# Delta inputs, first group: memsets ahead of the first gathers, second group's gathers behind the first group's power

## The reference, cut to what matters

```python
x = x + _L0_attn_ref(_layernorm(x, axis=-1), ...)
x = x + _L0_ffn_ref(_layernorm(x, axis=-1), ...)     # out = sum(weights * y of the 2 chosen experts)
x = x + _L1_attn_ref(_layernorm(x, axis=-1), ...)    # q, k, v = silu(short_conv(x @ Wq, ...)) and so on
x = x + _L1_ffn_ref(_layernorm(x, axis=-1), ...)
```

## Time and profile before

| | |
|---|---|
| median of 3 runs | 1436.7 us (1435.37 to 1441.69) |
| the profiled execution | 1436.34 us |
| its span, first to last instruction | 1434.6 us |
| busy in the span | TensorE 89%, VectorE 57%, GpSimd 35%, ScalarE 32% |
| clock granted to TensorE, mean | 0.916 of full speed |

### The profile page before, as it was taken

The page is one execution under the profiler, slowest core; times in us unless marked ns, Lnnn a source line. Parts: engine busy times, 40 slices in busy tenths (PEclk is TensorE's granted clock), DMA queues, the critical chain, the costliest instruction groups (busy, mean ns, idle before and its releaser), DMA issues. The chain is left out here.

```text
span 1434.6 us, 36334 instructions
## 1 busy us (share of the span) xinstructions
PE 1277.0 (89%) x12853; PEld 951.4 (66%) x12854; DVE 820.7 (57%) x1882; ACT 463.3 (32%) x1085; POOL 496.5 (35%) x709
## 2 busy tenths in 40 slices
PE   7999999899999999838888887298999999889997
PEld 5888888767776777614554555287888888746565
DVE  6788889533222222248888877457566666435443
ACT  1211222132222222226767774011222222123332
POOL 4344666415411111065666432223343434210000
PEclk9999999889999999968888997558999999779999
DMA  9999910113311211122444434612643334000001
GB/s 309 349 370 340 328 49 31 38 48 109 113 59 60 64 59 59 48 73 95 138 122 119 114 107 136 129 50 74 117 115 89 94 94 147 2 0 30 29 22 37
DMA packets 219962, 156.60 MB, mean 109 GB/s; under 512 B 111744, under 2 KB 201344, under 8 KB 219840
## 3 DMA queue, kind: packets, MB, share of 16 engines
q1 hardware_dynamic: 204288, 129.11, 30.7%
q0 software_dynamic: 9312, 25.44, 5.4%
q10 hardware_dynamic: 6240, 0.39, 0.3%
HBM read 64.47 MB, written 90.44 MB: 108 GB/s over the span
## 5 line engine op out<-in xcount | busy, mean ns | idle before, releaser
L945 PE MATMUL ps_sc<-w,a_qeo 128*128 x568 | 183.1, 466 | 0.0
L753 DVE TENSOR_TENSOR a_stm<-a_vpad,ps_sc 128x352 f32<-128x352 f32 x71 | 37.0, 521 | 177.2 <-ACT a_vpad L517 177.2
L945 PEld LDWEIGHTS ps_sc<-w,a_qeo 128*128 128x128 f32 x568 | 104.0, 193 | 46.5 <-issue 2.5
L423 POOL DMA_DIRECT2D x_slots<-a_stm x66 | 36.4, 551 | 226.1 <-issue 226.1
L1585 PE MATMUL d_pp<-d_xT,d_w_p 128*128 128x512 f32 x192 | 112.1, 732 | 1.1 <-ACT d_xT L1320 1.1
L1477 DVE SCALAR_TENSOR_TENSOR d_cout<-d_cin,d_taps,d_cout 128x512 f32<-128x512 f32 x144 | 106.1, 747 | 6.1 <-ACT d_cout L1338 2.7
L915 PE MATMUL ps_kv<-w,a_stm 128*128 x426 | 105.7, 384 | 1.2 <-DVE a_stm L746 1.1
L915 PEld LDWEIGHTS ps_kv<-w,a_stm 128*128 128x128 f32 x426 | 79.2, 190 | 30.1 <-issue 12.5
L2328 PE MATMUL g_pp<-g_xT,g_w_g 128*128 128x512 f32 x192 | 90.8, 613 | 8.3 <-ACT g_xT L2219 8.3
L1253 POOL DMA_INDIRECT got<-x_slots,d_idx x64 | 75.5, 1180 | 18.7 <-issue 16.1
L517 ACT ACTIVATE a_vpad<-ps_sc 128x352 f32<-128x352 f32 x71 | 33.0, 464 | 140.0 <-PE ps_sc L945 140.0
(11 more groups left out here) (273 smaller groups left out, 2834.4 us busy)
## 6 DMA issues: line engine op xcount, KB each, us to landing
x_slots<-a_zeros SPq DMA_DIRECT2D x32, 1024.0 KB, 11.0
rec<-d_kve SPq DMA_DIRECT2D x32, 384.0 KB, 2.9
u_kve<-rec SPq DMA_DIRECT2D x32, 384.0 KB, 3.9
a_qeo<-x_slots SPq DMA_DIRECT2D x71, 128.0 KB, 2.0
x_slots<-a_stm POOLq DMA_DIRECT2D x66, 128.0 KB, 2.1
rec<-d_act_out SPq DMA_DIRECT2D x32, 256.0 KB, 3.7
u_qkT<-rec SPq DMA_DIRECT2D x32, 256.0 KB, 3.5
w<-in_w SPq DMA_DIRECT2D x4, 1408.0 KB, 14.0
```

What stands on the lines that cost most here:

```text
L753: dve.tensor_tensor(e_h[:, q, 0:HID], e_gate[:, q, :], ps_3[q], ALU.mult).then_inc(h_out, 1)
L945: mm = pe.matmul(ps, e_xT[:, q, k, :], w13[:, s, k, bass.ds(e_hidden, 1), :], start=(k == 0), stop=(k == KD - 1))
```

## The change

Two things in GpSimd's program of `delta_inputs`. The four memsets stand ahead of the first group's index copy and gathers. And in step 0 the gathers of tiles 0 and 1 of group 1, with their index copy, stand behind the shift and the power of group 0; those of tiles 2 and 3 follow them as before (in step 0 nothing lies between). The later steps are as they were.

```diff
-            gather(0, 0, (0, 1, 2, 3))
             pool.memset(power[:, :, 0, :], -0.5).then_inc(zeroed, 1)
             pool.memset(power[:, :, 1, :], 0.5).then_inc(zeroed, 1)
             pool.memset(cin[:, :, :, 0:HIST], 0.0).then_inc(zeroed, 1)
             pool.memset(s_rows[:, 0:HIST], 0.0).then_inc(zeroed, 1)
+            gather(0, 0, (0, 1, 2, 3))
             pool.wait_ge(zeroed, 4)
 
             def step(i, par):
                 u, q = i - 1, 1 - par
                 v = i - 2
-                if has(i + 1, NG):
+                if i > 0 and has(i + 1, NG):
                     gather(i + 1, 1 - par, (0, 1))
                 if has(i, NG):
                     pool.wait_ge(mom_done, GROUP * (i + 1))
...
                     pool.tensor_scalar(shifted[:, :], mom[:, :, 1], EPS, None, ALU.add).then_inc(shift_done, 1)
                     pool.wait_ge(shift_done, i + 1)
                     pool.tensor_tensor(rstd[:, :], shifted[:, :], power[:, :, 0, 0], ALU.pow).then_inc(rstd_done, 1)
+                if i == 0:
+                    gather(1, 1, (0, 1))
```

## The result

The changed kernel took 1440.54 us in the median of 22 runs (1436.84 to 1443.86), the kernel before 1438.32 in 22 (1433.14 to 1442.64). The ratio is 1.0019, with a 95% interval of 1.0011 to 1.0027: 2.7 us slower, 1.6 to 3.9 (the two medians lie 2.2 apart). The forecast was 1439.4, or 2.7 us slower, and no difference that one measurement tells apart.

What follows compares the result with a forecast made beforehand. GpSimd's queue was taken to bound the restart: VectorE waits for group 1's eighth gather, whose landing moves from 635.55 to 638.21. That +2.66 us, with nothing absorbed, made the median 1439.4 us; range 1433.0 to 1446.5.

Steps and rivals of the forecast that it cites:

- The bound: At the start of delta inputs, GpSimd's gather queue is late; VectorE idles 5.60 us until group 1's eighth gather lands.
- The sum, term by term: GpSimd's queue to VectorE's adds of group 1: eighth gather starts at 635.35, lands at 638.21, against 635.55: 2.66 us later.
- The memsets: Four memsets ahead of group 0's gathers on GpSimd: first gathers move back by 0.34 us, with 0 as other bound.
- The gathers beside VectorE's adds: Group 0's late gathers on GpSimd, now running while VectorE adds, take 0.14 us more.
- The lead is lost: Group 0's normalisation comes 2.68 us earlier, but VectorE's late adds of group 1 hold up its convolutions, so nothing is gained.
- No slack behind: Behind VectorE's adds of group 1, nothing absorbs the delay: every later row of the stage comes 2.7 us later.
- The rule on contention: GpSimd gathers contend with VectorE's two-input instructions; by this rule savings and costs of moved gathers sum within 0.2 us.
- Lead kept: Rival, chance 0.14: VectorE's adds of group 1 don't bound the restart, group 0's 2.68 us carry to the end; 1434.0 us.
- absorbed: Rival, chance 0.11: a later join, such as the 3.87 us wait for the decay, absorbs the delay; 1436.7 us.
- Clock, slower: Rival, chance 0.13: shifted work meets one more drop of TensorE's clock, 7.0 us, giving 1446.4 us.
- clock, faster: Rival, chance 0.06: one drop of TensorE's clock vanishes, 7.0 us less, giving 1432.4 us.
- one dip: One stretch of lowered TensorE clock, priced at 7.0 us from matmul counts in 1000 to 1020 and the next 20 us.

Runs made afterwards that it cites:

- The wait by tile: Changed kernel, with VectorE waiting for group 1's gathers tile by tile instead of once for all eight; ratio to before 0.9969, and 0.9984 when measured again.
- the order alone: Kernel before, with only group 1's gathers of tiles 0 and 1 moved behind group 0's power, memsets left in place; ratio to before 1.0035.
- the pure delay: Kernel before, with a GpSimd memset of 3072 elements per partition and a wait for it ahead of the first gathers; ratio to before 1.0010.
- the memsets alone: Kernel before, with only the four memsets moved ahead of group 0's gathers, group 1's gathers in their old order; ratio to before 0.9983.

## Why the prediction held

*The bound.* Read from rows 3 and rows 4: VectorE's wait ends with the eighth gather of group 1. The row of after names the DMA again, for 10.58 us, and 637.72 is 2.83 behind the start of the eighth gather at 634.89 (2.86 before).

*The sum, term by term.* The mechanism held, and the closeness of the terms is in part luck, since two errors of opposite sign nearly cancel. The memsets were put at 0.34 us; they delay the first gather by 0.14 (+0.93 in place of +0.79). The four and the start of the copy take 0.20, since instructions of 0.10 to 0.14 us overlap, and the gap between copy and gather shrinks a little; the value lay between the bounds 0 and 0.34. The gathers beside VectorE's adds were put at 0.14 more and cost 0.25 (610.19 to 619.32 is 9.13, not 8.88), nearly all in the one at 615.33, 1.18 us, which runs beside VectorE's work on tile 0. The delay of 0.20 us too much and the 0.11 too little nearly cancel: eighth gather predicted at +10.15 (619.80), measured +10.06. Fourth tile's add +13.01, measured +13.02. Shift +14.75, measured +14.88. First gather of group 1 +16.58, measured +16.69; the eighth +25.70, measured +25.63. Adds of group 1 +28.56, measured +28.46. The delay was predicted as 2.66 and is 2.56 in the first pair of profiles, 2.49 in the second.

*The lead is lost.* Right, and on the path named, ScalarE's waits for VectorE's convolutions. It starts to be lost two waits earlier than the one at 654.73 that the prediction named: the first is at 643.22. The wait by tile shows its cause directly.

*No slack behind.* Right in rows: a delay of 2.40 us arrived whole at the shift of group 2, and the 5.33 us of the order alone as well. In time it is shown only within 1.5 us or so. Behind group 2 the rows don't show it as cleanly. From its shift to the delta rule the second profile of before took 248.97 us, the pure delay 249.99, the changed kernel 250.06 and 250.13, the order alone 250.55, but the memsets alone, which are early, 249.75 as well. Whether a delay grows there by about 1 us is open.

*The rule on contention.* The prediction read two of the four gathers beside group 0's adds in before (0.98 and 0.94 us) and left out this one:

```profile
622.36 1.11 POOL L1253 DMA_INDIRECT got<-x_slots,d_idx  x1 [0.30 <-issue]
```

So of the eight gathers beside these adds in the two kernels, two took 1.11 and 1.18 us and the others 0.94 to 0.98. The Trainium skill (GPSIMD Engine Reference, section 8, Key points) names this contention; beside the adds the runs show at most 0.25 us of it in the sum. Elsewhere in the stage gathers take longer. In before, the first two behind the decay of group 0 lie beside VectorE's two-input product (line 1513) and its scan (line 1519):

```profile
649.01 2.05 POOL L1253 DMA_INDIRECT got<-x_slots,d_idx  x1 [0.17 <-issue]
...
651.37 1.87 POOL L1253 DMA_INDIRECT got<-x_slots,d_idx  x1 [0.30 <-issue]
```

That is about 1 us more for each, off the path here. The product (648.88, 1.23 us) ends at 650.11, 1.10 us after the first of them starts, and that gather took 1.10 us more than 0.95. This fits a gather that is held up until the product ends, but no run tests it, and the adds, which have two inputs as well, held up most gathers hardly at all.

*The rivals.* "Lead kept" and "absorbed" fell. "Clock, slower" and "clock, faster" did not decide the totals of many runs. The two shown profiles do differ by 7.0 us, the price that the prediction gave one dip, but that is chance: 2.6 of it is the door, and 3.1 lie in the pattern of the later steps, for which the granted clock isn't shown as the cause: it was 1.00 in both profiles in the step with the largest piece, and its mean was higher in the longer one. The price itself is too high by its own row: 20 us at a granted 0.76 give 4.8 us less of full clock, and the rest of the difference in counts isn't shown to be the clock.

*The range.* The 2.7 us of the ratio agree with the sum of 2.66 better than the measurement is good (1.6 to 3.9), and the medians give 2.2; so close an agreement is luck. The forecast of 1439.4 is 1.1 below the measured median, since before rose by 1.6 us with the larger sample (1436.7 to 1438.32).

## What to carry to other kernels

When work is moved behind a wait on an in-order queue, the queue pays the idle time of the wait once more for everything behind it, also for the next group; look for who waits for the last of it, and for every other consumer (here the decay) that the moved work now stands ahead of. An early first group is worth nothing while its consumer sits behind one wait for the whole second group: divide the wait first, and then the order is worth moving, here by about 1 us. Compare stages from their own first instruction, and profile the unchanged kernel twice, also on the chip of the changed one, before a difference far from the edit is given to the edit.

## What the runs showed of the hardware

Four small memsets in a row, 0.11, 0.11, 0.14 and 0.10 us long in the rows, take 0.20 us together up to the next instruction, since their rows overlap. The first gather of the stage stood 0.79 us behind the start of its index copy, 0.73 with 0.20 us of memsets ahead of both, but 0.46 when a memset of 2.66 us and a wait for it lay ahead. And one program ran through the groups behind group 2 in steps of 32.2 to 32.4 us, or in steps of which most were 31.0 to 31.5, up to 5.5 us apart in the stage (+308.19 against +302.71, on two chips), which is twice what the change costs. The longer pattern went with idle time of 0.2 to 0.5 us, once or twice, inside TensorE's row of 128 small matmuls, at a granted clock of 1.00 in the step that was compared.
